# Routed rows that carry their gates, are scaled in the expert stage and are summed by accumulating gathers

## The reference

```python
probs = sigmoid(x @ router_w.T + expert_bias)
top_w, top_idx = jax.lax.top_k(probs, 8)
top_w = 2.5 * top_w / (sum(top_w) + 1e-9)
combine[t, top_idx] = top_w
h1 = silu(einsum('th,eih->eti', x, w_gate))
routed = einsum('eti,ehi->th', h1 * combine.T[:, :, None], w_down)
shared = silu(x @ w_gate_shared.T) @ w_down_shared.T
```

## Time and profile before

| | us |
|---|---|
| median of three runs | 4009.31 |
| profiled execution, time | 4020.27 |
| its span, first to last instruction | 4018.8 |
| first half of the attention | about 1440 |
| experts | about 550 |
| second half of the attention | about 1640 |

### The profile page before, as it was taken

How to read it: one execution, slowest core, us unless ns; L and a number is a source line. 1 busy time by engine, 2 the same in 40 slices (tenths; PEclk the granted TensorE clock), 3 DMA queues, 4 the chain that set the end, 5 groups by cost and what they waited for, 6 DMA issues and landing times. The chain is left out here.

```text
span 4018.8 us, 64097 instructions
## 1 busy us (share of the span) xinstructions
PE 2553.6 (64%) x20970; PEld 1289.1 (32%) x20970; DVE 3233.2 (80%) x4350; ACT 2511.9 (63%) x1684; POOL 2458.5 (61%) x1748
## 2 busy tenths in 40 slices
PE   5661556666667666667888864566656666665566
PEld 3440112322223222246677641122222222222224
DVE  6886998999998999833333359999999999999993
ACT  1110978887878887743333337777777777777773
POOL 2222887778786786813333457677777677776762
PEclk9885978998888888878999988778878787878886
DMA  7883122322222222126888851222222222222222
GB/s 257 305 307 99 37 75 68 110 68 77 75 67 83 92 81 71 59 77 202 240 240 241 245 175 32 63 70 75 66 74 67 74 66 75 64 75 67 75 60 82
DMA packets 376226, 445.80 MB, mean 111 GB/s; under 512 B 49185, under 2 KB 291697, under 8 KB 376050
## 3 DMA queue, kind: packets, MB, share of 16 engines
q1 hardware_dynamic: 293106, 283.77, 22.5%
q0 software_dynamic: 58752, 148.46, 11.3%
q10 hardware_dynamic: 24192, 11.02, 1.0%
HBM read 239.08 MB, written 204.02 MB: 110 GB/s over the span
## 5 line engine op out<-in xcount | busy, mean ns | idle before, releaser
L1093 DVE SCALAR_TENSOR_TENSOR u_dve<-s_win,rpos,ps_here 128x512 f32<-128x512 f32 x1792 | 1226.7, 739 | 155.7 <-PE ps_here L1176 71.8
L1193 PE MATMUL ps_l<-u_dve,wsel 128*32 128x512 f32 x6144 | 955.3, 746 | 570.4 <-ACT u_dve L1003 337.9
L947 POOL TENSOR_TENSOR u_pool<-s_win 128x4096 f32<-128x4096 f32 x128 | 1021.4, 7980 | 15.6 <-PE ps_l L1193 12.9
L1003 ACT ACTIVATE u_dve<-u_dve 128x4096 f32<-128x4096 f32 x224 | 809.7, 3615 | 217.6 <-DVE u_dve L1093 217.1
L1088 DVE TENSOR_TENSOR u_dve<-s_win,ps_here 128x4096 f32<-128x4096 f32 x160 | 703.2, 4410 | 0.0
L926 POOL DMA_INDIRECT xslot_dram<-xr,slot_now x512 | 509.0, 994 | 151.4 <-issue 146.6
L935 POOL DMA_INDIRECT yg<-yslot_dram,slot_now x512 | 496.2, 969 | 164.6 <-issue 144.1
L1001 ACT ACTIVATE u_dve<-u_dve,bdmg_sb 128x4096 f32<-128x4096 f32 x128 | 474.6, 3708 | 152.6 <-DVE u_dve L1088 152.3
L1193 PEld LDWEIGHTS ps_l<-u_dve,wsel 128*32 128x32 f32 x6144 | 206.1, 125 | 997.8 <-issue 566.0
L1001 ACT ACTIVATE u_pool<-u_pool,bdmg_sb 128x4096 f32<-128x4096 f32 x128 | 473.8, 3701 | 38.6 <-POOL u_pool L947 38.6
L1386 DVE TENSOR_TENSOR hs<-sg,ps_e 128x512 f32<-128x512 f32 x168 | 115.5, 688 | 382.9 <-ACT sg L1371 382.9
(11 more groups left out here) (143 smaller groups left out, 3324.1 us busy)
## 6 DMA issues: line engine op xcount, KB each, us to landing
band<-band_dram SPq DMA_DIRECT2D x32, 2048.0 KB
xslot_dram<-zero SPq DMA_DIRECT2D x16, 2688.0 KB, 10.1
xs<-xslot_dram SPq DMA_DIRECT2D x168, 256.0 KB, 3.6
yslot_dram<-ys POOLq DMA_DIRECT2D x168, 256.0 KB, 3.3
band_dram<-ml SPq DMA_DIRECT2D x64, 512.0 KB
we<-in_w_expert SPq DMA_DIRECT2D x336, 64.0 KB, 2.8
s_win<-s_dram SPq DMA_DIRECT2D x64, 288.0 KB, 8.2
s_dram<-s_sb POOLq DMA_DIRECT2D x16, 1024.0 KB, 4.6
```

The lines of the kernel that those rows point to most:

```text
L947: pool.tensor_tensor(item_buffer(n), windows(par, ty, d0, 8), s_win[:, par, ty, PAD:PAD + TC].unsqueeze(1).to_broadcast([P, 8, TC]), ALU.s ...
L1003: act.activation(u, u, ACT.Gelu).then_inc(gelu_done, 1)
L1093: last = dve.scalar_tensor_tensor(out=item_buffer(n)[:, d, :], in0=s_win[:, par, ty, d0 + d + 1:d0 + d + 1 + TC], scalar=rpos[:, d0 + d:d0 ...
L1193: last = pe.matmul(ps_l[32 * g:32 * g + 32, cgrp % 2, ty, :], wsel[:, ty, q, :], item_buffer(n)[:, d, :], start=(q == 0), stop=(q == 3))
```

## The change

The gate of each routed row travels with the row. Rows of `xslot_dram` get 129 columns. In the first half ACT loads each block of 128 rows eight times side by side from `xn_dram` (`load_rows`, one load a block, four a step) and copies the block's eight gates into the 129th columns; POOL scatters as before, from that copy. In the experts DVE scales each tile's output by the gate as it leaves PSUM, in four instructions instead of one; the buffer of rows is now held until then, so SP's load waits for `ys_ready`. In the second half POOL gathers straight into `acc`, adding on the way, in eight rounds of four blocks, two gathers behind each item; each waits until the round before has landed in its block. `add_routed`, `yg`, `gate_now` and the gates on ACT go. The base rows are loaded a step earlier. DVE normalises in both halves; POOL's L963 goes.

```diff
-        xslot_dram = dram("xslot_dram", (NSLOT, C))
+        xslot_dram = dram("xslot_dram", (NSLOT, C + 1))
...
-                                         zero[:, 0:ZR * C // 3].unsqueeze(1).to_broadcast([P, 3, ZR * C // 3]))\
+                                         zero[:, 0:ZR * (C + 1) // 3].unsqueeze(1)
+                                         .to_broadcast([P, 3, ZR * (C + 1) // 3]))\
...
-                xr = sb("xr", [P, 2, J, C], F32, c)
+                xr = sb("xr", [P, 2, TOPK, C + 1], F32, c)
             else:
-                yg = sb("yg", [P, NS, C], F32, c)
-                gate_now = sb("gate_now", [P, 2, NS], F32, c)
                 acc = sb("acc", [P, 2, J, C], F32, c)
...
                     def store_routed(t, par):
 
-                        if some(NS * (t - 1)):
-                            sp.wait_ge(sum_round, NS * (t - 1))
+                        for j in range(J):
+                            sp.wait_ge(gathered[j], 16 * TOPK * (t - 1))
                             sp.sem_inc(held, 1)
...
-                        sp.dma_start(acc[:, 1 - par], chunk_rows(part_dram, t - 1)).then_inc(base_in, 16)
+                        sp.dma_start(acc[:, par], chunk_rows(part_dram, t)).then_inc(base_in, 16)
...
+                    def scatter(s, par, j):
 
                         pool.wait_ge(slots_here, s + 1)
                         pool.sem_inc(held, 1)
+                        pool.wait_ge(rows_in[j % 2], 16 * (2 * s + j // 2 + 1))
+                        pool.sem_inc(held, 1)
+                        pool.wait_ge(gates_here, J * s + j + 1)
+                        pool.sem_inc(held, 1)
+                        for k in range(TOPK):
+                            i = j * TOPK + k
+                            pool.indirect_dma_start(
+                                xslot_dram, bass.IndirectOffsetOnAxis(ap=slot_now[:, par, i:i + 1], axis=0),
+                                xr[:, j % 2, k, :], None).then_inc(scattered[j % 2], 16)
+
+                    def gather(s, par, n):
+
+                        if n == 0:
+                            pool.wait_ge(slots_here, s + 1)
                             pool.sem_inc(held, 1)
+                            pool.wait_ge(base_in, 16 * (s - first + 1))
+                            pool.sem_inc(held, 1)
+                        k = n // 2
+                        for j in (2 * (n % 2), 2 * (n % 2) + 1):
+                            if some(16 * (TOPK * (s - first) + k)):
+                                pool.wait_ge(gathered[j], 16 * (TOPK * (s - first) + k))
                                 pool.sem_inc(held, 1)
+                            i = j * TOPK + k
+                            pool.indirect_dma_start(
+                                acc[:, par, j, :], None, yslot_dram,
+                                bass.IndirectOffsetOnAxis(ap=slot_now[:, par, i:i + 1], axis=0),
+                                compute_op=ALU.add).then_inc(gathered[j], 16)
...
-                            if half == 1 and "s" in st and n == 15:
-
-                                pool.wait_ge(inv_in, s)
-                                pool.tensor_tensor(ml[:], ml[:], winv[:].unsqueeze(2).to_broadcast([P, J, D, HH]),
-                                                   ALU.mult).then_inc(normed, 1)
-                            if "i" in st and n % 4 == 3:
-                                route(s, par, n // 4)
+                            if half == 0 and "i" in st and n % 4 == 3:
+                                scatter(s, par, n // 4)
+                            if half == 1 and "i" in st:
+                                gather(s, par, n)
...
+                    def load_rows(s, j):
+
+                        done = 16 * TOPK * (2 * s + j // 2)
+                        if some(done):
+                            act.wait_ge(scattered[j % 2], done)
+                            act.sem_inc(held, 1)
...
+                        rows = xn_dram[bass.ds(s * TC + j * P, P), :]
+                        act.dma_start(xr[:, j % 2, :, 0:C], rows.unsqueeze(1).to_broadcast([P, TOPK, C]))\
+                            .then_inc(rows_in[j % 2], 16)
+                        act.activation(xr[:, j % 2, :, C:C + 1],
+                                       gates_all[:, bass.ds(s * NS + j * TOPK, TOPK)].unsqueeze(2), ACT.Copy)\
                             .then_inc(gates_here, 1)
...
-                            if half == 1 and "i" in st and n == 6:
-                                gates(s, par)
+                            if half == 0 and "i" in st and n % 4 == 1:
+                                load_rows(s, n // 4)
...
-                                        if sums:
-                                            if d == 7:
-                                                last.then_inc(sub_dve, 1)
-                                            add_routed(s - first, 1 - par, 2 * n + d)
-                                if not sums:
-                                    last.then_inc(sub_dve, 1)
+                                last.then_inc(sub_dve, 1)
...
-                                if half == 0:
-                                    dve.wait_ge(inv_in, s)
-                                    dve.tensor_tensor(ml[:], ml[:], winv[:].unsqueeze(2).to_broadcast([P, J, D, HH]),
-                                                      ALU.mult).then_inc(normed, 1)
+                                dve.wait_ge(inv_in, s)
+                                dve.tensor_tensor(ml[:], ml[:], winv[:].unsqueeze(2).to_broadcast([P, J, D, HH]),
+                                                  ALU.mult).then_inc(normed, 1)
...
-            xs = sb("xs", [P, BUF, TB, C], F32, c)
+            xs = sb("xs", [P, BUF, TB, C + 1], F32, c)
...
-                            sp.wait_ge(rows_turned, n - (BUF - 1))
+                            sp.wait_ge(ys_ready, n - (BUF - 1))
...
-                        dve.tensor_copy(ys[:, u].rearrange("p i (h c) -> p h i c", h=2),
-                                        ps_z[:, u % 2, :, 0:TB * I].rearrange("p h (i c) -> p h i c", i=TB))\
-                            .then_inc(ys_ready, 1)
+                        for i in range(TB):
+                            last = dve.tensor_scalar(ys[:, u, i, :].rearrange("p (h c) -> p h c", h=2),
+                                                     ps_z[:, u % 2, :, i * I:(i + 1) * I], xs[:, u, i, C:C + 1],
+                                                     None, ALU.mult)
+                        last.then_inc(ys_ready, 1)
```

More of the change, by code:

```diff
@@ L666, in moe_attention_layer @@
         here_done = sem("here_done")
-        rows_in, slots_here = sem("rows_in"), sem("slots_here")
+        rows_in, slots_here = [sem(f"rows_in{u}") for u in range(2)], sem("slots_here")
         scattered = [sem(f"scattered{u}") for u in range(2)]
@@ L856, in routed @@
                             store_routed(t, par)
-                        if some(t):
-                            load_base(t, par)
+                        load_base(t, par)
                     def chunk(b, tc, it):
@@ L974, in _ @@
                 def _(act):
-                    def gates(s, par):
-                        if some(NS * (s - first - 1)):
-                            act.wait_ge(sum_round, NS * (s - first - 1))
-                        act.activation(gate_now[:, par], gates_all[:, bass.ds((s - first) * NS, NS)], ACT.Copy)\
+                    def load_rows(s, j):
[3 more added lines that the diff above has]
+                            act.sem_inc(held, 1)
+                        if some(16 * (2 * s + j // 2)):
+                            act.wait_ge(rows_in[j % 2], 16 * (2 * s + j // 2))
+                            act.sem_inc(held, 1)
+                        rows = xn_dram[bass.ds(s * TC + j * P, P), :]
[3 more added lines that the diff above has]
+                                       gates_all[:, bass.ds(s * NS + j * TOPK, TOPK)].unsqueeze(2), ACT.Copy)\
                             .then_inc(gates_here, 1)
@@ L1043, in bring @@
                         if half == 0:
-                            if some(16 * NS * it):
-                                dve.wait_ge(scattered[par], 16 * NS * it)
-                        else:
-                            if some(NS * (s - first - 1)):
-                                dve.wait_ge(sum_round, NS * (s - first - 1))
+                            if some(2 * 16 * TOPK * (s - 1) if some(s) and some(s - 1) else 0):
+                                for u in range(2):
+                                    dve.wait_ge(scattered[u], 2 * 16 * TOPK * (s - 1))
+                        else:
+                            if some(s - first - 1 if some(s - first) else 0):
+                                for j in range(J):
+                                    dve.wait_ge(gathered[j], 16 * TOPK * (s - first - 1))
                         dve.tensor_copy(slot_now[:, par], slots_all[:, bass.ds((s - first) * NS, NS)])\
```

(19 more changed lines are left out.)

38 lines of the change are left out of this document (6 added, 32 removed).

## The result

The changed kernel takes 3965.84 us (median of five runs, 3962.95 to 3977.39). The ratio of its runs to those of the kernel before is 0.990, with a 95% interval of 0.988 to 0.992: 1% faster, where 4.6% was forecast; this is 6 us above the top of the range. The profiled execution's span is 3965.2 us.

What follows compares the result with a forecast made beforehand. VectorE was taken as busiest, with POOL close behind after the change at an 84.5 us step; second half -205, first half +15, experts +5 make -185 us, forecast 3825 us, range 3735 to 3960.

Steps and rivals of the forecast that it cites:

- The bound before and what leaves it: Second half: VectorE's 97.2 us step loses 20.6 us of row sums; with normalisation and blocking added, 80.6 us.
- POOL's price of an adding gather: Second half: 0.075 us over a plain gather's 1.25 us, 2.4 us a step; upper end +0.97 us each.
- the same sum: POOL's second-half step: 72.8 us kept, plus 3 for waiting before spreading, 2 for gathers' waits, 2.4 for adding: 80.2 us.
- the allowance for waits: Second half, POOL: some 32 more wait and counter steps at 0.06 us each, 2 us a step, ends 0 and 5.
- The landing: Second half: a gather lands in 2.5 us, 3.2 at most; even doubled, just covered by the 5.0 us of four gathers.
- The first two steps: Second half, VectorE's first item to first normalisation: 169.9 us before, taken as 145, so -25 us.
- The tail: End of the second half: the last normalisation falls from 4.5 us and a hand-over to 2.3 us, so -2.5 us.
- Blocked instructions: Second half, VectorE: averages for instructions POOL's subtraction can catch, +3.4 us for normalisation and +2.1 us for the first L1133.
- The first half: ScalarE's four loads and gate copies a step make VectorE wait, +1.1 us a step, 14 steps: +15 us.
- The experts: 516-byte rows may land later: +5 us, ends 0 and +38; four scalings add 0.7 us a batch on an unsaturated engine.
- dearer gathers: Rival, second half: 0.3 us more per gather, POOL at 90, step 91 us, 3920 us in all; chance 0.17.
- the slower rival: Second half: accumulating issue makes POOL the bound, tipping at 0.55 us more a gather; issue done twice, 4275 us; chance 0.13.

Runs made afterwards that it cites:

- the kernel with visible landings: Changed kernel with a block's eight rounds one behind another, so each gather waits for the landing of the one just before: 4912.1 us in one run.

## Why the prediction was wrong

**The bound before and what leaves it**: right. With plain gathers the step was 85.0 us by the count and 82.8 by the starts of the normalisations, where I had put 84.5; first to last normalisation 1203 us, where I had 1230; and the time 3781 us, below the forecast of 3825.

**The term that failed is POOL's price of an adding gather.** I took 0.075 us more than a plain one, from the slope between POOL's plain transfers, and kept the whole issue twice, +0.97, as the upper end. It is +0.61. With it the same sum gives 72.8 + 3 + 32 x 0.61 = 95.3 us without the allowance for waits; measured 95.7, or 94.8 by the starts. That it fits so well is partly luck: the 3 us were for a wait before the spreading that the steady steps do not have, and in their place stand the gathers that VectorE holds up (2 us) and what is uncertain in the rest. The slope was the wrong neighbour: it prices rows added to an ordinary transfer, and nothing in it shows what adding costs.

By the profiled executions the change was to bring -185 us and brought -54. Of the 131 us missing, first to last normalisation holds 143 (-178 forecast, -35 measured), the first two steps 24 and the experts with their surroundings 5; the first half gave 38 back and the tail 3. The first two of these are POOL's price: with plain gathers both came out at or below the forecast. Two of the signs that I had set for being wrong appeared, a gathers' mean above 1.3 us (1.61) and the normalisation above 6 us (8.9, in the second half alone); the third, idle time before gathers released by transfers, is there too but is almost all the 0.30 us gap.

**The waits of their own for each gather** cost nothing: the gap is 0.30 us with and without them; I had 2 us a step. **The landing** was hidden, as said: 3.3 us behind 5.6.

**The first two steps** were to shrink by 25 us to 145 and stayed at 169, since POOL paces them from the first gather on; with plain gathers they took 139.5. **The tail** gave 5.3 us for 2.5.

**Blocked instructions.** I used averages (3.4 and 2.8 us). Neither is a constant: the normalisation's mean was 2.3 to 8.9 us, by where POOL's subtraction falls. Which engine binds does not settle it. It was 7.4 us with VectorE as the bound, and in the kernel with visible landings, where POOL is the bound and waits, it was never caught:

```profile
L1120 DVE TENSOR_TENSOR ml<-ml,winv x32: 2291/2292/2309, 523.6 to 4858.9; 128x2048 f32<-128x2048 f32 x32
```

Moved in the kernel before, it cost 101 us. In the changed kernel VectorE has the time, but the gather behind it is held up for 1.87 us on POOL, 28 us over the 15 steps where that happened. The prediction had no such term.

**The first half**: forecast +15, measured -20 in the profiled executions; the loads on ScalarE did not show, and fewer instructions were caught. First half and experts together, forecast at +20, came to -6 us over ten runs. **The experts**: forecast +5, measured +10, most of it (some 8 us, one profile) from the scalings that I had put at nothing, though VectorE was busy for only half of the stage.

**The rivals.** In time, reality fell between "dearer gathers" (3920 us) and no gain. In price it lies at the tipping point of the slower rival. I had put that at +0.55 us, 1.8 instead of 1.25, but counted it from a step of 80.2 us that already held 0.075 us a gather; over a plain gather it is +0.62, and "1.8 instead of 1.25" should read 1.87. For the same reason the doubled issue would give 109 us a step and not 111, and the 52 us in that rival's sum have no working. At the measured +0.61 the kernel is still 1% faster, because the waits were free and the first half with the experts cost nothing instead of 20 us. The chance that I gave to both, 0.30 together, was too small for a price that no row held.

## What to carry to other kernels

When work is moved onto an engine in an instruction form that the trace does not hold, its price decides, and the nearest row of another form is no estimate of it; measure that form first, and compute the count of instructions at which the engine becomes the bound. Look at every other engine's step time with the candidate's work taken off: here POOL was at 77 us of 97, and 32 instructions at 0.6 us more were all of its slack. The sums on VectorE were slow more for what they collided with than for their arithmetic: 40 of the 512, the caught ones, hold 203 of their 364 us. One reduction for each block, with a single SBUF operand, did the same work in less than half the time. And a collision is to be priced on both engines: the one that waits first holds up the other afterwards.

## What the runs showed of the hardware

- An indirect gather of 128 rows with addition took 1.55 us on POOL against 0.94 without, the same at 64 and at 128 columns, and landed in 3.3 us against 2.5; the queue counted 112 packets more for each, also at 64 columns.
- A VectorE multiplication on two SBUF operands that met POOL's subtraction ended 2.16 us after it, whenever it had started: up to 9.4 us for one of 2.3. POOL's adding gather that started meanwhile ended 1.42 us after the multiplication, and took 3.42 us instead of 1.55. The multiplication's minimum, median and maximum:

```profile
L1120 DVE TENSOR_TENSOR ml<-ml,winv x32: 2291/2340/9411, 523.9 to 3917.0; 128x2048 f32<-128x2048 f32 x32
```

- A reduction over a strided SBUF operand took 1.9 ns an element on VectorE and ran at the same length beside POOL's subtraction.
